# First expert loop: nine pairs fetched early by SyncE, waits for the last scatters moved, expert 8 split ahead of the loop, and two address lines in the table

## What is computed

```python
def moe(x, norm_w, gate_w, gate_b, w1, b1, w2, b2):   # x is layernormed, 2048 tokens
    t = x * rsqrt(mean(x * x) + 1e-5) * norm_w
    vals, idx = top_k(t @ gate_w.T + gate_b, 4)        # 16 experts
    G[token, idx] = softmax(vals)
    h = einsum('mh,eoh->emo', t, w1) + b1              # 512 hidden columns, pairs (a, b)
    act = min(a, 7) * sigmoid(1.702 * min(a, 7)) * (clip(b, -7, 7) + 1)
    y = einsum('emi,edi->emd', act, w2) + b2
    return x + einsum('me,emd->md', G, y)
x = x + 0.5 * moe(layernorm(x));  x = x + attention(layernorm(x));  x = x + 0.5 * moe(layernorm(x))
```

## Time and profile before

| | us |
|---|---|
| median of three runs | 806.88 (803.91 to 807.64) |
| the profiled execution, its own time | 807.14 |
| its span in the trace | 804.4 |
| TensorE busy | 702.1 (87%) |
| VectorE busy | 586.4 (73%) |
| ScalarE busy | 440.1 (55%) |
| GpSimd busy | 403.1 (50%) |

### The profile page before, as it was taken

The page is one execution under the profiler, slowest core; times in us unless marked ns, Lnnn a source line. Parts: engine busy times, 40 slices in busy tenths (PEclk is TensorE's granted clock), DMA queues, the critical chain, the costliest instruction groups (busy, mean ns, idle before and its releaser), DMA issues.

```text
span 804.4 us, 18633 instructions
## 1 busy us (share of the span) xinstructions
PE 702.1 (87%) x4754; PEld 556.0 (69%) x4754; DVE 586.4 (73%) x1360; ACT 440.1 (55%) x1066; POOL 403.1 (50%) x449
## 2 busy tenths in 40 slices
PE   2576757899999999789999999988699999999995
PEld 2453436678788888666677777656478888888872
DVE  3868365977677777647778988867777777777777
ACT  3664434655555555426777676755245555555551
POOL 6667763445545555463235532447425555555552
PEclk9999879999999999999999999999899999999998
DMA  7949897768986553264444334147656877886776
GB/s 299 388 191 365 300 374 263 241 189 289 330 271 217 205 188 117 85 247 167 157 158 165 142 143 152 58 171 248 219 174 219 272 260 261 272 279 201 230 255 242
DMA packets 77919, 181.06 MB, mean 225 GB/s; under 512 B 12016, under 2 KB 36864, under 8 KB 73856
## 3 DMA queue, kind: packets, MB, share of 16 engines
q1 hardware_dynamic: 38176, 94.44, 34.3%
q0 software_dynamic: 14928, 49.97, 16.6%
q10 hardware_dynamic: 24720, 35.47, 13.6%
HBM read 97.60 MB, written 65.45 MB: 203 GB/s over the span
## 4 chain that ended last, share of the span: by engine, by line
PE 30%; issue 8%; POOL 8%; DVE 8%; DMA 1%; ACT 1%; ACTq 0%; DVEq 0%; POOLq 0%
PE s_psT L1149 7%; POOL kbuf L1361 5%; PE s_psG L1173 3%; PE s_psS L1700 3%; PE s_psO L1735 3%; DVE s_a_nm L1968 3%; PE s_psG L1672 2%; POOL rows L1593 2%; POOL s_e_own_bc L1373 1%; PE s_psT L1716 1%; PE s_psG L1685 1%; PE s_psS L1116 1%; PE s_psT L1720 1%; PE s_psS L1130 1%; DMA rows<-s_a_row,s_a_slot_i 1%
## 5 line engine op out<-in xcount | busy, mean ns | idle before, releaser
L1361 POOL DMA_INDIRECT kbuf<-f_e_ys,f_e_place x79 | 80.4, 1018 | 100.9 <-ACT f_e_ys L1308 84.6
L1149 PE MATMUL f_bank<-weights,f_e_th 128*128 x316 | 120.3, 479 | 6.7 <-issue 3.5
L1361 POOL DMA_INDIRECT kbuf<-s_e_own_ys,s_e_own_place x79 | 79.2, 1003 | 92.0 <-ACT s_e_own_ys L1308 79.4
L1149 PE MATMUL s_psT<-s_e_own_weights,s_e_own_th 128*128 x316 | 114.4, 464 | 2.9 <-ACT s_e_own_th L1333 2.1
L1593 POOL DMA_INDIRECT rows<-s_a_row,s_a_slot_i x64 | 63.8, 996 | 75.8 <-DVE s_a_slot_i L2095 58.9
L1968 DVE TENSOR_REDUCE s_a_nm<-s_psS 128x4 f32<-128x1024 f32 x64 | 78.2, 1222 | 26.3 <-PE s_psS L1700 25.7
L1214 DVE TENSOR_TENSOR s_e_own_hb<-s_psT,s_e_own_bias 128x512 f32<-128x512 f32 x79 | 54.3, 687 | 48.3 <-PE s_psT L1149 48.2
L1214 DVE TENSOR_TENSOR f_e_hb<-f_bank,f_e_bias 128x512 f32<-128x512 f32 x79 | 54.2, 686 | 43.4 <-PE f_bank L1149 43.2
L714 POOL DMA_INDIRECT rows<-f_r_row,f_r_slot_i x64 | 66.1, 1033 | 34.1 <-issue 17.9
L1149 PEld LDWEIGHTS f_bank<-weights,f_e_th 128*128 128x128 f32 x316 | 62.3, 198 | 29.9 <-issue 11.8
L2234 ACT ACTIVATE s_a_pT<-s_psT 128x1024 f32<-128x1024 f32 x62 | 63.4, 1022 | 30.5 <-PE s_psT L1720 30.0
(11 more groups left out here) (396 smaller groups left out, 1801.8 us busy)
## 6 DMA issues: line engine op xcount, KB each, us to landing
s_e_own_weights<-w_split SPq DMA_DIRECT2D x12, 1024.0 KB, 5.4
s_e_tb<-rows ACTq DMA_DIRECT2D x80, 144.0 KB, 3.2
w_split<-weights ACTq DMA_DIRECT2D x7, 1536.0 KB, 6.2
...
weights<-w_raw SPq DMA_DIRECT2D x10, 768.0 KB, 13.7
w_split<-weights POOLq DMA_DIRECT2D x5, 1536.0 KB, 7.7
...
```

Source lines behind the costliest of these rows:

```text
L1149: last = pe.matmul(psH[j][:, :], left[:, p % 2, j, k * P:(k + 1) * P], weights[:, h:len_units + h - SLOT + 1, k * I2:(k + 1) * I2][:, bass ...
L1361: pool.indirect_dma_start(out=kbuf[:, :], out_offset=bass.IndirectOffsetOnAxis(ap=place[:, i % KEPT:i % KEPT + 1], axis=0), in_=ys[:, n, : ...
```

## The change

- SyncE fetches nine pairs (`EARLY` 9) and goes through all of them before it turns to expert 4's weights. The loads of experts 11 and 12 stand behind the fetches of pairs 4 and 6 (`SP_LOADS`).
- A tile of `need` 3 no longer waits for stage 2 of `s_landed` but for stage 1 and the whole count of the last rank's semaphore; other tiles wait for that semaphore to be at least 16. GpSimd and the count no longer wait for the last scatters. GpSimd waits for them only ahead of expert 13's load, at step 5 (before at step 4). All padding is waited for by SyncE ahead of pair 0. ScalarE's waits for scatters stand ahead of pair 9, at step 5.
- Four scatters of ranks 2 and 3 are sent between the groups (`SENT_BETWEEN`).
- Expert 8 is split ahead of the loop: by ScalarE behind its padding, by VectorE behind expert 3. Experts 9 and 10 move up a step, as do the stores of 8, 9 and 10.
- The table has one line for the first weights' address and one for the second's, each as expert * 64 + address, and TensorE loads both. The semaphores `s_ready1` and `s_ready2` count in 64s, so that an entry can be waited for as it stands. The second block has only the expert's number in the table, and places its weights evenly, 3 units each.
- Register loads of more than eight entries are cut into pieces.

```diff
@@ -33,7 +33,8 @@
-NEED, EARLY = 3 * NT + 2 * NE + TOP * RINGS, 7
+NEED, EARLY = 3 * NT + 2 * NE + TOP * RINGS, 9
+SPOT2 = NEED + 2 * EARLY
@@ -44,18 +45,20 @@
+SPOT_BITS, TURN, SECOND_RING = 6, 100, 5 * SLOT
...
-    base = RING_AT if first_layer else 0
-    return [(HOMES[e], HOMES[e] + 2) if first_layer and e in HOMES else (base + SLOT * (e % 4), base + SECOND_UNITS[e % 5]) for e in range(NE)]
...
-def packed(first_layer):
...
-    return [e + (first << 5) + (second << 10) for e, (first, second) in enumerate(spots(first_layer))]
+    if not first_layer:
+        return [(SLOT * (e % 4), SLOT * (e % 5) + 2) for e in range(NE)]
+    return [(HOMES[e], HOMES[e] + 2) if e in HOMES else (RING_AT + SLOT * (e % 4), RING_AT + SECOND_UNITS[e % 5]) for e in range(NE)]
...
+def packed(part):
...
+    return [(e << SPOT_BITS) + spot[part] for e, spot in enumerate(spots(True))]
@@ -303,8 +306,6 @@
-        if stage == TOP - 2:
-            engine.wait_ge(self.s_pad[1], 16 * (NE - FIRST))
@@ -369,18 +376,24 @@
-def tile_lines(one, table, psN, more, first):
...
-    for k, to in enumerate((0, NT, 2 * NT + 2 * NE)):
-        one.done(one.engine.tensor_scalar(table[0:1, to:to + NT], psN[0:1, k * P:k * P + NT], float(first) if k == 1 else 0.0, None, ALU.add))
-    one.done(one.engine.tensor_scalar(table[0:1, NEED:NEED + 2 * EARLY], psN[0:1, 3 * P:3 * P + 2 * EARLY], more, None, ALU.add))
+def tile_lines(one, table, psN, more, by_group):
...
+    line = lambda k, n: psN[0:1, k * TURN:k * TURN + n]
+    one.done(one.engine.tensor_copy(table[0:1, 0:NT], line(0, NT)))
+    if by_group:
+        one.done(one.engine.tensor_copy(table[0:1, NT:2 * NT], line(1, NT)))
+    else:
+        one.done(one.engine.tensor_scalar(table[0:1, NT:2 * NT], line(1, NT), float(packed(0)[0]), None, ALU.add))
+        one.done(one.engine.tensor_scalar(table[0:1, SPOT2:SPOT2 + NT], line(4, NT), float(packed(1)[0]), None, ALU.add))
+    one.done(one.engine.tensor_copy(table[0:1, 2 * NT + 2 * NE:3 * NT + 2 * NE], line(2, NT)))
+    one.done(one.engine.tensor_scalar(table[0:1, NEED:NEED + 2 * EARLY], line(3, 2 * EARLY), more, None, ALU.add))
...
-def tile_turns(pe, c, tiles, psN):
...
-    for k, name in enumerate(("off", "spot", "col", "need")):
-        last = pe.transpose(psN[0:1, k * P:(k + 1) * P], tiles[name][:, :], c["ident"][:, :])
+def tile_turns(pe, c, tiles, psN, by_group):
...
+    for k, name in enumerate(("off", "te", "col", "need") if by_group else ("off", "spot1", "col", "need", "spot2")):
+        last = pe.transpose(psN[0:1, k * TURN:k * TURN + NT], tiles[name][0:NT, :], c["ident"][0:NT, 0:NT])
@@ -538,6 +552,7 @@
+    SENT_BETWEEN = (((0, 2), (0, 3)), (), ((1, 2), (2, 2)), (), ())
@@ -676,16 +691,17 @@
-                tile_columns(one, c, tiles, hist[:, LAST + 1, :], None, c["steps"][:, 0, :])
+                tile_columns(one, c, tiles, hist[:, LAST + 1, :], None, c["steps"])
...
-        tile_lines(one, table, psN, 0.0, packed(True)[0])
+        tile_lines(one, table, psN, 0.0, False)
...
+        split.low(dve, 8)
@@ -725,12 +741,14 @@
+            for n, k in SENT_BETWEEN[g]:
+                send(n, k)
...
-            for n in range(TT):
+            left = [n for n in range(TT) if not any((n, k) in some for some in SENT_BETWEEN)]
+            for n in left:
...
-                if n == 1:
+                if n == left[1]:
...
-        routed.landed(pool, 2)
@@ -805,6 +823,7 @@
+        split.high(act, 8)
@@ -998,15 +1025,15 @@
-    HIGH_AT = {(-1, 0): ((8, 0),), (-1, 1): ((8, 1), (8, 2)), (0, 0): ((9, 0),), (0, 1): ((9, 1), (9, 2)),
-               (1, 0): ((10, 0),), (1, 1): ((10, 1), (10, 2)), (2, 0): ((11, 0),), (2, 1): ((11, 1), (11, 2)),
-               (4, 0): ((12, 0),), (4, 1): ((12, 1), (12, 2)), (6, 0): ((13, 0),), (6, 1): ((13, 1), (13, 2)),
+    HIGH_AT = {(-1, 0): ((9, 0),), (-1, 1): ((9, 1), (9, 2)), (0, 0): ((10, 0),), (0, 1): ((10, 1), (10, 2)),
+               (2, 0): ((11, 0),), (2, 1): ((11, 1), (11, 2)), (4, 0): ((12, 0),), (4, 1): ((12, 1), (12, 2)),
+               (6, 0): ((13, 0),), (6, 1): ((13, 1), (13, 2)),
...
-    LOW_AT = {(-1, 1): ((8, 0),), (0, 0): ((8, 1), (8, 2), (9, 0)), (1, 0): ((9, 1), (9, 2)), (1, 1): ((10, 0),),
-              (2, 0): ((10, 1),), (2, 1): ((10, 2), (11, 0)), (3, 0): ((11, 1),), (3, 1): ((11, 2),),
+    LOW_AT = {(-1, 1): ((9, 0),), (0, 0): ((9, 1),), (0, 1): ((9, 2), (10, 0)), (1, 0): ((10, 1),), (1, 1): ((10, 2),),
+              (2, 1): ((11, 0),), (3, 0): ((11, 1),), (3, 1): ((11, 2),),
...
-    ACT_STORES, POOL_STORES, POOL_LOADS, SECOND_LAG = {1: 8, 2: 9, 3: 10}, {16: 11, 19: 12, 22: 13, 25: 14, 28: 15}, {4: 13, 6: 14, 8: 15}, 2
+    ACT_STORES, POOL_STORES, POOL_LOADS, SP_LOADS, SECOND_LAG = {0: 8, 1: 9, 2: 10}, {16: 11, 19: 12, 22: 13, 25: 14, 28: 15}, {5: 13, 6: 14, 8: 15}, {4: 11, 6: 12}, 2
@@ -1016,7 +1043,13 @@
-            queue.wait_ge(routed.s_landed, need[j])
+            if first_layer:
+                third = queue.snap(need[j] & (need[j] >> 1)).with_bounds(min_val=0, max_val=1)
+                queue.wait_ge(routed.s_landed, (need[j] >> 1) + 1)
+                carry(queue, s_carry)
+                queue.wait_ge(routed.s_scat[TOP - 2], third * (16 * (T // P - 1)) + 16)
+            else:
+                queue.wait_ge(routed.s_landed, need[j])
@@ -1028,21 +1061,36 @@
-            sp.sem_inc(s_ready2, 1)
+            sp.sem_inc(s_ready2, ready_by(e))
...
-            sp.load(needs, table[0:1, NEED:NEED + 2 * BY_SP])
-            landed = [sp.snap(r, min_val=1, max_val=TOP - 1) for r in needs]
+            bounded = lambda some: [sp.snap(r, min_val=1, max_val=TOP - 1) for r in some]
+            sp.load(needs[0:4], table[0:1, NEED:NEED + 4])
+            landed = bounded(needs[0:4])
...
+            routed.other_rows(sp)
...
+            for first in range(4, 2 * BY_SP, 8):
+                last = min(first + 8, 2 * BY_SP)
+                sp.load(needs[first:last], table[0:1, NEED + first:NEED + last])
+                landed += bounded(needs[first:last])
+            for p in range(2, BY_SP):
+                early_fetch(sp, at, p, landed[2 * p:2 * p + 2], s_carrys)
+                if p in SP_LOADS:
+                    split.load(sp, SP_LOADS[p])
+            at.free()
+            for register in needs:
+                sp.free_register(register)
...
-        sp.load(begins, table[0:1, 2 * NT + NE + 1:2 * NT + NE + 1 + NE - NBUF + 1])
+        for first in range(0, len(begins), 8):
+            some = begins[first:first + 8]
+            sp.load(some, table[0:1, 2 * NT + NE + 1 + first:2 * NT + NE + 1 + first + len(some)])
@@ -1072,14 +1120,6 @@
-        if BY_SP:
-            for p in range(2, BY_SP):
-                early_fetch(sp, at, p, landed[2 * p:2 * p + 2], s_carrys)
-            at.free()
-            for register in needs:
-                sp.free_register(register)
-            split.load(sp, 11)
-            split.load(sp, 12)
@@ -1102,7 +1142,8 @@
-        expert = Column(pe, "e", NT, most)
+        expert = Column(pe, "e", NT, most1)
+        second_spot = Column(pe, "e2", SPOT2, most2) if first_layer else expert
@@ -1132,13 +1173,30 @@
+        def first_of(h, k):
...
+            if first_layer:
+                return weights[:, h:UNITS + h - SLOT + 1, k * I2:(k + 1) * I2]
+            return weights[:, 0:NBUF * SLOT, :].rearrange("p (s u) n -> p s u n", u=SLOT)[:, :, h, k * I2:(k + 1) * I2]
...
+        def second_of(h, k):
...
+            at = (1 - h) * I2 + k * D
+            if first_layer:
+                return weights[:, :, at:at + D]
+            return weights[:, :, :].rearrange("p (s u) n -> p s u n", u=SLOT)[:, :, SLOT - 1, at:at + D]
...
-                at = pe.snap((spot >> 5) & 31).with_bounds(min_val=0, max_val=len_units - SLOT)
-                pe.wait_ge(s_ready1, (spot & 31) + 1)
+                if first_layer:
+                    at = pe.snap(spot & ((1 << SPOT_BITS) - 1)).with_bounds(min_val=0, max_val=UNITS - SLOT)
+                    pe.wait_ge(s_ready1, spot)
+                else:
+                    at = pe.snap(spot % NBUF)
+                    pe.wait_ge(s_ready1, spot + 1)
@@ -1159,9 +1217,13 @@
-            spot = expert(i)
-            at = pe.snap(spot >> 10).with_bounds(min_val=0, max_val=len_units - 1)
-            pe.wait_ge(s_ready2, (spot & 31) + 1)
+            spot = second_spot(i)
+            if first_layer:
+                at = pe.snap(spot & ((1 << SPOT_BITS) - 1)).with_bounds(min_val=0, max_val=UNITS - 1)
+                pe.wait_ge(s_ready2, spot)
+            else:
+                at = pe.snap(spot % NSEC)
+                pe.wait_ge(s_ready2, spot + 1)
@@ -1363,6 +1432,8 @@
+            if first_layer and s == min(POOL_LOADS):
+                routed.rows(pool)
```

70 lines of the change are left out of this document (45 added, 25 removed).

## The result

The changed kernel took **813.09 us** (median of 5 runs, 811.4 to 814.14). The kernel before took 806.88 beside it, so the ratio is 1.0066, with a 95% interval of 1.0044 to 1.0088: 0.7% slower. The forecast was 793.5, faster, in a range of 788 to 802. It was wrong in its sign. The profiled execution took 812.07 us, with a span of 809.8.

What follows compares the result with a forecast made beforehand. The prediction took the loop's body to be bound by TensorE and its start by chains of waits. From 807.14 us it took 15.1 for pair 7 turning earlier and added 1.5 for register loads: 793.5 us, range 788 to 802.

Steps and rivals of the forecast that it cites:

- TensorE's registers: First loop: two table loads every four pairs in place of one, taken to cost 1.5 us, between 0 and 5.5.
- The steps at every fourth pair are over 6 us: First loop, where TensorE loads its registers: a sign that would show the forecast wrong.
- Rival 4: First loop's register loads: both taking 1.96 us would cost 3.15 us a block, 820 us in all; chance 0.05.
- SyncE's new wait for all pads hides under that.: Loop's start: the first fetch moves by 1 to 2.5 us, hidden under pair 0 turning 1.4 us later.
- The 3.15 us go.: Loop's start: with pairs 2 to 4 fetched early, pair 2's 3.15 us wait for its rows disappears.
- rival 1: Loop's start: transfers bind, scatters land at 124.3, pair 7 turns at 127.6, time 797 us; chance 0.16.
- The scatters, and expert 11: Loop's start: GpSimd's landing wait ends at 98.5, scatters land by 120.8, ScalarE's 8.31 us wait for expert 11's weights goes.
- ScalarE's 7.98 us for `ys`: Loop's start: ScalarE's 7.98 us wait, its pair 7 fetch standing behind all scatters, goes as SyncE waits instead.
- Expert 8 ahead: 1.4 us later, in the loop nothing.: Expert 8 split ahead of the loop: pair 0 turns 1.4 us later, nothing on balance in the loop.
- The 793.5 itself: Whole kernel: the forecast time of 793.5 us, with pair 7 turning at 124.1; chance 0.58.

Runs made afterwards that it cites:

- x3: The changed kernel with TensorE reading one table line again, the second address packed above the first, no second load: 795.14 us, ratio 0.9839.
- x1: The changed kernel with the second table line begun two entries later, at byte 1296 in place of 1288: 797.79 us, ratio 0.9883.
- x5: x3 with SyncE waiting for the pads of experts 4 to 15 behind its fetches of pairs 0 and 1: 793.02 us, ratio 0.9829.
- x7: x5 with SyncE issuing expert 10's load behind its fetch of pair 2 instead of ahead of it: 792.79 us, ratio 0.9822.
- x9: x5 with the loads of experts 11 and 12 issued behind all nine fetches: 873.49 us, ratio 0.995, in jobs with the kernel before at 876 and 880.
- x8: x5 with GpSimd waiting again for the last scatters' landing ahead of its first put: 792.64 us, ratio 0.9804.
- x10: x5 with seven early pairs in place of nine: 862.49 us, ratio 0.9819, in jobs with the kernel before at 876 and 880.
- x6: x5 with ScalarE's split of expert 8 moved behind the last gates, still before the pair loop: 792.54 us, ratio 0.9815.
- x11: x5 with expert 8 split inside the pair loop again: 866.06 us, ratio 0.9868, in jobs with the kernel before at 876 and 880.

## Why the prediction was wrong

- **"TensorE's registers: I take 1.5 us, between 0 and 5.5."** This is the step that failed. The second line's load costs 17.9 us as the change has it (changed kernel less x3), of which 15.3 are its place (less x1) and about 2.7 the load itself, the term I had meant to size (the 2.7 lie within the noise of the two runs). I took the earlier trace rows as one population, and "up to 1960" as its rare upper end; its members all came from lines at multiples of 16 bytes, and the added one does not. The entry where it begins was in the diff: 304 + 18 = 322. That a long load shows as idle time was in the prediction, by the earlier trace rows; its duration was mis-sized.
- **"The steps at every fourth pair are over 6 us"** was a poor sign of being wrong: in the kernel before three of the eight (to pairs 9, 13 and 21: 7.7, 6.9 and 6.6 us) were over 6 already.
- **Rival 4** had the mechanism and 0.05 of the chances. By its own formula, with the measured durations: 0.59 + 1.95 - 0.77 = 1.77 us a block, just over the 1.7 at which it turns against the change, times nine 16 us. The sum would have been 807.1 - 15.1 + 16 = 808; the 5 us to the measured 813 are about what pair 7 lacks for other reasons (it turned at 130.1 in x3, not at 124.1). I priced it with both loads slow (820) and weighed it by the median, which no badly placed load has.
- The Trainium skill (DMA: Bandwidth & Descriptors, Latency and other measured facts) gives a floor of about 600 ns for such a load; the well placed ones come down to it (587 to 592 ns in about half of them). The badly placed one is over three times that. The Trainium skill also says (Advanced Engine Details and Errata, SBUF Cachelines) that SBUF has cachelines of 16 bytes, and that accesses to a different line each cost more; eight entries from byte 1288 touch three such lines, from 1296 two, counted from the table's start. That fits what x1 shows, but two and three lines alone would not make three times the time, and no run here shows the mechanism.
- By the 64 deep queue of TensorE that I cited from the Trainium skill (TensorE: Matmul & The Clock Gate, Architectural detail) both loads could have been hidden. 16.4 us of "issue" speak against it, as the 1.19 us of the earlier trace rows had.
- **"SyncE's new wait for all pads hides under that."** Wrong, and the smaller slip: the first fetch moved 3.94 us and not up to 2.5, since ScalarE's last pads went out until 79.51 where I had taken 78.2. x5 against x3 gives 4.2 us at pair 7, as pair 2's rows come late behind it too, and 2.1 in time, within the noise.
- **"The 3.15 us go."** Half right: pair 2 waited 1.04 us in the changed kernel, but 5.17 in x1 and 5.75 in x3. The rows stand behind expert 10's load on SyncE, beside expert 8's store. x7 shows that moving the load only moves the wait, from pair 2 to pair 3. To that extent the transfers hold this stretch, as rival 1 had it. Its own term did not come: the scatters didn't land at 124.3, as SyncE could fetch pair 7 at 118.1 to 121.2 us. That pair 7 at 125.9 to 130 lies around its 127.6 is chance.
- **The scatters, and expert 11.** Right in place and, within 2 us, in size: the landing wait ended at 100.4 (98.5), SyncE fetched pair 7 at 121.2 (120.8), ScalarE's 8.31 us went, and x9, which puts the load behind the fetches again, has 7.17 in that place.
- **ScalarE's 7.98 us for `ys`** went too, as forecast. x8 and x10, where its longest wait there is 1.6 and 1.5 us, don't take back what removed it: in x8 SyncE still fetches pair 7, and in x10 the scatters were there before.
- **"Expert 8 ahead: 1.4 us later, in the loop nothing."** 1.1 us in x6, and covered by pair 7; for the loop x11 shows nothing beyond the noise.
- **The 793.5 itself.** x5 comes to 793.02, but it has no second load, and for it the sum would be 792.0. Pair 7 is 1.8 us later than forecast. The agreement to half a microsecond is partly luck: the six runs of x5 lie between 787.93 and 796.14.
